# Quantised rows turned by SyncE's DMA transposes, context chunks moved ahead of the evictions, two LoRA tiles ahead of the coefficients

## The chip, the cores and the metric

One NeuronCore of one Trainium2 chip runs the whole kernel. The metric is the device time of one execution in microseconds; three runs of the kernel before give a median of 1277.35 us (1276.79 to 1277.54). The profile below is of one execution, with its own time.

## The reference, cut to what matters

`x` is 2 x 512 rows of 1024, `ctx` is 2 x 1024 rows of 1024. Four steps follow one another; the change lies in the first two.

```python
q1 = fake_quant(layernorm(x), s1, z1)          # (clip(round(x/s + z), 0, 255) - z) * s
q2 = fake_quant(ctx, s2, z2)                   # here ctx stands as a 1024 x 1024 matrix for each batch
x = x + tanh(g_xattn[0]) * (q1 @ q2)
y = layernorm(x)
coeffs = softmax((y.mean(1) @ Wq.T) @ lora_keys.T / sqrt(128))
h = einsum('bsi,eir->bser', y, lora_down)
x = x + tanh(g_ffn[0]) * (y @ W_org.T + einsum('be,bser,ero->bso', coeffs, h, lora_up))
x = x + tanh(g_xattn[1]) * cross_attention(layernorm(x), ctx)   # 32 query heads, 8 key/value heads
x = x + tanh(g_ffn[1]) * two_of_three_experts(layernorm(x))
```

## The kernel before

Each engine has an instruction list written out by hand, and semaphores tie the lists together. An engine takes its list strictly in order, so an instruction that waits holds up all that stand behind it. There are TT = 8 token tiles of 128 rows, TB = 4 for each of the B = 2 batches, and KT = 8 slices of the contraction.

**Front, first part (0 to about 97 us).** TensorE computes the attention's keys and values of both batches from the transposed context (`keys_values`, 16 passes, each raises `kv_step`), in all eight PSUM banks. The context arrives in 32 chunks (`CHUNKS`): T chunks are the transposed context for the keys, split into a bf16 high part (ScalarE, line 1078) and low part (VectorE, L1353); N chunks are the natural context, scaled by ScalarE (L1080), clipped and rounded by VectorE into `Q2` (L1398 and L1400). A ring of six buffers holds them, two in `stage_c` and four in the space of `XTh`; SyncE loads a chunk once the one six places before it is done (`c_done`, L364). Between the chunks VectorE normalises and quantises the eight x tiles (`x_step`, `quantise_x`) into `XQ`, which is the space of `XTl`; ScalarE takes roots (L1086), scales (L1090) and sums each row of `XQ` (`row_sum`, L1097). After batch 0 and batch 1 both engines evict the banks (`kv_out`: ScalarE L1103 and L1106, VectorE L1412 and L1417). In ScalarE's list chunks 26 and later, and in VectorE's list chunks 28 to 31, stand about or behind `kv_out(1)`, and ScalarE's `add_rows` (L1110, adds the row term to x) stand between chunks.

**Front, second part (to about 218 us).** TensorE turns every quantised tile with eight 128x128 transposes into bank 6 or 7 (`turn_quantised`, L694, `xq_turned`); ScalarE copies it to `XTh` (`quantised_out`, L1115, `xq_t`). `column_sums` (L686) multiplies `Q2` by ones in banks 4 and 5; VectorE's `column_terms` (L1496) scales this into `CB`, and GpSimd's `add_columns` (L539) adds it to x (`x_pre`). `quantised_tile(t)` (L718, 16 matmuls) computes q1 q2 for one token tile in banks 0, 1 or 2, 3 (`nat_mm`). VectorE's `quantised_update(t)` adds it to x (L1513, `x_up`), takes the statistics of the new row (L1366, L1371) and the inverse root (L1379 to L1385) and leaves `ln_bias`; ScalarE's `scale_rows(t)` writes the normalised rows (L1196); TensorE's `turn_behind(t)` transposes them into banks 4 and 5 (L706); ScalarE's `turned_out(t)` (L1202) and VectorE's `lo_parts(t)` (L1503) split them into `XTh` and `XTl`. `lo_parts(t-2)` stands inside `quantised_update(t)`, and `turn_behind(t)` waits for `lo_parts(t-1)`, since both use banks 4 and 5.

The adapters follow: `lora_query` (24 matmuls), `lora_scores`, VectorE's `lora_shares` with one Exp on ScalarE, `lora_spread` (L739) and the copy into `cvec` give the coefficients; `lora_hidden(u)` (24 matmuls) gives the eight hidden tiles, which ScalarE and VectorE scale with them (L1214, L1552). Before the change only `lora_hidden(0)` stands ahead of `lora_spread(0)`.

GpSimd splits weights into high and low parts (L507 and L509, one pair for each 128x1024 slice, `wt_done`), in the order of `WT_LAYOUT`: four slices of down, eight of org, four of up, then q and o. SyncE feeds it through two staging buffers (L354). The token tiles of the second step (`token_tile`) start when the up and org slices are split.

Of the kernel before, what the change touches and what calls it, by code (L numbers as in the profile page):

```python
# [42 lines left out]
WT_LAYOUT = [("kv", 4), ("down", 4), ("org", 8), ("up", 4), ("q", 8), ("o", 8)]  # L43
# [15 lines left out]
H_BANK = (7, 6, 7, 6, 1, 6, 7, 2)  # L59
# [57 lines left out]
def build(nc, x, ctx_nat, ctx_t, wts, lora_q, lora_keys, scalars, gate_w, w1, b1, w2, b2, out):  # L117
    with ExitStack() as ctx:
# [65 lines left out]
        XQ = XTl  # L184
        ring = [st[:, :] for st in stage_c] + [XTh[:, :].bitcast(F32)[:, i * D:(i + 1) * D] for i in range(RING - 2)]
# [60 lines left out]
        xq_turned = sem("xq_turned")  # L246
        xq_t = sem("xq_t")
# [100 lines left out]
        def _(sp):  # L348
# [147 lines left out]
        def _(pool):  # L496
# [127 lines left out]
        def _(pe):  # L624
# [58 lines left out]
            def column_sums(b):  # L683
                for h in range(2):
                    for k in range(KT):
                        mm = pe.matmul(bank[4 + h][:, :], onesb[:, :],  # L686
                                       Q2[b][:, k * D + h * HALF:k * D + (h + 1) * HALF], start=k == 0, stop=k == KT - 1)
                mm.then_inc(cs_mm, 1)

            def turn_quantised(t):  # L690
                if t >= 2:
                    pe.wait_ge(xq_t, t - 1)
                for k in range(KT):
                    mm = pe.transpose(bank_b[6 + t % 2][:, k * P:(k + 1) * P], XQ[:, t * D + k * P:t * D + (k + 1) * P],  # L694
                                      identb[:, :])
                mm.then_inc(xq_turned, 1)
# [14 lines left out]
            def quantised_tile(t):  # L711

                pe.wait_ge(xq_t, t + 1)
                if t >= 2:
                    pe.wait_ge(x_up, 2 * (t - 1))
                for h in range(2):
                    for k in range(KT):
                        mm = pe.matmul(pair(t)[h][:, :], XTh[:, k * D + t * P:k * D + (t + 1) * P],  # L718
                                       Q2[t // TB][:, k * D + h * HALF:k * D + (h + 1) * HALF],
                                       start=k == 0, stop=k == KT - 1)  # L720
# [55 lines left out]
            pe.wait_ge(xq_t, TT)  # L776
            lora_query(0)
            quantised_tile(TT - 1)
            turn_behind(TT - 3, 1)
            lora_scores(0)  # L780
            pe.wait_ge(wt_done, WT_AT["org"])
# [7 lines left out]
            lora_hidden(2)  # L789
            pe.wait_ge(h_lo, 2)  # L790
            lora_hidden(3)
            pe.wait_ge(x_up, 2 * TT)
            lora_query(1)
            lora_hidden(4)
            lora_scores(1)
            pe.wait_ge(h_lo, 4)
            lora_hidden(5)
            lora_spread(1)
            lora_hidden(6)
# [265 lines left out]
        def _(act):  # L1065
# [47 lines left out]
            def quantised_out(t):  # L1113
                act.wait_ge(xq_turned, t + 1)
                act.activation(per_tile(XTh)[:, :, t * P:(t + 1) * P],  # L1115
                               bank_b[6 + t % 2].rearrange("p (k n) -> p k n", k=KT), ACT.Copy).then_inc(xq_t, 1)


# [25 lines left out]
            scale_x(4)  # L1144
            kv_out(0)
            chunks(9, 10)
            row_sum(3)
            root(5, 1)
            chunks(10, 12)
            scaled(5)  # L1150
            chunks(12, 15)
            root(6, 0)
            chunks(15, 17)
            scaled(6)
            chunks(17, 19)
            root(7, 1)
            chunks(19, 20)
            scaled(7)
            chunks(20, 22)
# [9 lines left out]
            act.wait_ge(c_done, len(CHUNKS))  # L1169
# [53 lines left out]
            scale_rows(1)  # L1223
            for t in range(2, TT):
                turned_out(t - 2)
                scale_rows(t)
            lora_exp(0)
# [115 lines left out]
        def _(dve):  # L1343
# [131 lines left out]
            chunks(8, 9)  # L1475
            kv_out(0)
            chunks(9, 10)
            x_step(5)
            chunks(10, 15)
            x_step(6)  # L1480
            chunks(15, 19)
            x_step(7)
            chunks(19, 22)
# [400 lines left out]
```

## Time and profile before

| | us |
|---|---|
| median of the runs shown | 1277.35 |
| the profiled execution's own time | 1272.04 |
| its span, first to last instruction | 1270.2 |
| TensorE busy in the span | 1224.8 |

The profiled execution is 5.3 us shorter than the median, and 1.8 us of its time lie outside its span. TensorE is busy for 96% of the span. In the slices of 20 us it is busy 19.9 us in nearly every one from 180 us on; the slices with less lie in the front. An idle time in the timeline is printed behind the instruction that ended it, with what released it. Durations of one form are nearly constant, so a difference of two start times is the safest measure of a step.

### The profile page before, as it was taken

To read this page: it belongs to the slowest core of one execution; us is meant where nothing else is said; L and a number is where in the kernel's file an instruction comes from. 1 tells how busy PE (TensorE), PEld (TensorE's weight loads), DVE (VectorE), ACT (ScalarE), POOL (GpSimd) and SP (SyncE) were. 2 spreads that over 40 slices of the span, in tenths; PEclk is the share of its full clock that TensorE was granted. 3 is DMA by queue.
4 is the path that set the end of the run, shared out by engine and by line. 5 is a ranking of instruction groups with operands and counts; after the bars stand their busy time and mean duration, and the time that the engine had idled before them with its cause. 6 is when DMAs were issued, how large, how long until landed. Compare 5 with 4: busy or idle time off the path is not lost.

```text
span 1270.2 us, 16963 instructions
## 1 busy us (share of the span) xinstructions
PE 1224.8 (96%) x6485; PEld 518.0 (41%) x6568; DVE 821.0 (65%) x1417; ACT 483.9 (38%) x834; POOL 682.2 (54%) x300
## 2 busy tenths in 40 slices
PE   8997889999999999999999999999999999999998
PEld 6564444444444322222222222234444444444444
DVE  7877941333355678999899998516547855737622
ACT  4569321000011266777677767752253010010000
POOL 6004994900023387988889889980074553534510
PEclk9998989999999999999999999999999999999999
DMA  9464232411252334545454545343484342533301
GB/s 354 145 198 149 77 123 67 117 34 34 52 153 75 92 86 86 119 105 118 87 115 108 111 94 107 79 88 60 107 205 123 117 149 91 176 98 100 116 11 55
DMA packets 78317, 139.11 MB, mean 110 GB/s; under 512 B 40608, under 2 KB 50848, under 8 KB 74144
## 3 DMA queue, kind: packets, MB, share of 16 engines
q1 hardware_dynamic: 37392, 91.93, 22.7%
q0 software_dynamic: 4608, 33.56, 13.1%
q10 hardware_dynamic: 36240, 12.60, 5.0%
q8 instruction: 49, 0.80, 0.3%
q14 instruction: 28, 0.23, 0.1%
HBM read 85.49 MB, written 10.49 MB: 76 GB/s over the span
## 4 chain that ended last, share of the span: by engine, by line
PE 70%; DVE 12%; issue 2%; ACT 2%; DMA 2%; POOL 2%; ACTq 0%; SPq 0%; POOLq 0%; DVEq 0%
PE bank L631 45%; PE bank L881 9%; DVE mxp L1624 7%; PE bank L868 6%; PE bank L950 5%; PE bank L913 4%; DVE xn L1614 2%; POOL R L597 1%; PE bank L718 1%; DMA XTh<-xn 1%; DMA stage_pair<-R 1%; DVE XTl L1503 1%; DVE X L1513 0%; POOL stage_pair L597 0%; ACT R L1303 0%
## 5 line engine op out<-in xcount | busy, mean ns | idle before, releaser
L1624 DVE TENSOR_REDUCE mxp<-bank 128x1 f32<-128x512 f32 x512 | 320.5, 679 | 60.3 <-PE bank L868 60.0
L1269 ACT ACTIVATE R<-bank 128x512 f32<-128x512 f32 x512 | 273.9, 602 | 116.5 <-PE bank L950 113.2
L631 PE MATMUL bank<-XTh,R 128*128 128x512 bf16 x875 | 273.8, 382 | 1.9 <-DVE X L1672 1.1
L597 POOL TENSOR_TENSOR R<-R 128x2048 f32<-128x2048 f32 x48 | 218.6, 4555 | 36.5 <-ACT R L1269 34.8
L631 PE MATMUL bank<-R 128*128 128x512 bf16 x941 | 208.2, 379 | 1.0
L631 PE MATMUL bank<-XTl,R 128*128 128x512 bf16 x440 | 167.9, 382 | 2.1 <-ACT R L1327 1.4
L619 POOL TENSOR_TENSOR R<-stage_pair,R 128x1024 bf16<-128x1024 f32 x32 | 75.7, 2380 | 141.7 <-DVE R L1778 84.8
L631 PEld LDWEIGHTS bank<-R 128*128 128x128 bf16 x960 | 93.9, 98 | 113.3
L868 PE MATMUL bank<-R 96*128 96x512 bf16 x352 | 134.6, 382 | 4.7 <-DVE mxp L1624 3.0
L881 PE MATMUL bank<-R,stage_c 128*32 128x512 f32 x1024 | 137.1, 607 | 0.7 <-ACT R L1269 0.7
L950 PE MATMUL bank<-R 98*128 98x512 bf16 x352 | 134.4, 382 | 2.5 <-ACT R L1269 2.2
L631 PEld LDWEIGHTS bank<-XTh,R 128*128 128x128 bf16 x896 | 88.1, 98 | 109.7 <-issue 3.0
L507 POOL TENSOR_TENSOR R<-stage_pair,zero 128x1024 f32 (+1 forms) x35 | 67.2, 1920 | 91.1 <-DMA stage_pair<-wts_in 75.0
L619 POOL TENSOR_TENSOR R<-stage_c,R 128x1024 bf16<-128x1024 f32 x32 | 74.1, 2326 | 54.7 <-DVE R L1778 50.2
L1327 ACT ACTIVATE R<-bank,b1t 128x512 f32<-128x512 f32 x32 | 21.6, 686 | 198.3 <-PE bank L631 198.3
L868 PEld LDWEIGHTS bank<-R 96*128 96x128 bf16 x352 | 34.2, 97 | 112.2 <-DVE mxp L1624 85.5
L509 POOL TENSOR_TENSOR R<-stage_pair,R 128x1024 f32 (+1 forms) x35 | 75.9, 2168 | 5.3 <-POOL R L507 4.7
L1614 DVE RECIPROCAL xn<-p_total 128x128 f32<-128x128 f32 x64 | 59.2, 936 | 29.1 <-POOL xn L579 29.1
L597 POOL TENSOR_TENSOR stage_pair<-R 128x2048 f32<-128x2048 f32 x16 | 73.6, 4601 | 4.3 <-ACT R L1269 3.2
L913 PE MATMUL bank<-R,XTh 128*128 128x512 bf16 x250 | 69.5, 384 | 1.0 <-issue 0.8
L1823 DVE SCALAR_TENSOR_TENSOR X<-xn,TV,X 128x512 f32<-128x512 f32 x32 | 67.4, 2146 | 0.1
L1804 DVE CAST R<-R 128x512 bf16<-128x512 f32 x32 | 17.5, 547 | 74.9 <-ACT R L1327 74.9
(197 smaller groups left out, 1504.3 us busy)
## 6 DMA issues: line engine op xcount, KB each, us to landing
stage_pair<-wts_in SPq DMA_DIRECT2D x35, 512.0 KB, 3.6
R<-R POOLq DMA_DIRECT2D x16, 1024.0 KB, 7.0
stage_pair<-R POOLq DMA_DIRECT2D x16, 1024.0 KB, 7.0
stage_pair<-w_in SPq DMA_DIRECT2D x32, 512.0 KB, 3.6
stage_c<-w_in SPq DMA_DIRECT2D x32, 512.0 KB, 3.6
R<-q_scr SPq DMA_DIRECT2D x48, 128.0 KB, 2.4
XTh<-ctx_t_in SPq DMA_DIRECT2D x11, 512.0 KB, 7.6
XTh<-ctx_nat_in SPq DMA_DIRECT2D x9, 512.0 KB, 4.5
```

What stands on the lines that cost most here:

```text
L509: pool.tensor_tensor(lo, stage_w[stage][:, :], hi, ALU.subtract).then_inc(wt_done, 1)
L597: pool.tensor_tensor(PS[(0, 1, 2, 1)[j]], PB[2 * j % 4], PB[2 * j % 4 + 1], ALU.add).then_inc(p_add, 1)
L619: pool.tensor_tensor(lo[:, cols], stage_e[(n - N_WT) % RING_E][:, :], hi[:, cols], ALU.subtract).then_inc(wt_done, 1)
L631: mm = pe.matmul(o, a, m, start=first and a is ah and bs is bh, stop=last and a is al)
L868: pe.matmul(bank[s_bank(u)][:, :], QS[g % 3][0:96, h * S + qt * P:h * S + (qt + 1) * P], KS[g % 3][0:96, kh * HALF:(kh + 1) * HALF], start ...
L881: mm = pe.matmul(out_bank[h * HD:(h + 1) * HD, :], weights, probs[:, h * S:(h + 1) * S], start=first, stop=last)
L913: mm = pe.matmul(outs[h], a[i][:, cols], b[i][:, k * D + h * HALF:k * D + (h + 1) * HALF], start=k == 0 and i == 0, stop=k == KT - 1 and i ...
L950: pe.matmul(bank[t_bank(g, t)][:, :], KS[g % 3][0:98, kt * P:(kt + 1) * P], QS[g % 3][0:98, h * S:(h + 1) * S], start=True, stop=True).the ...
L1269: act.activation(PB[kt % 4][:, h * S:(h + 1) * S], bank[t_bank(g, t)][:, :], ACT.Exp, scale=float(HD) ** -0.5).then_inc(exp_done, 1)
L1614: dve.reciprocal(rec[:, cols], p_sum[:, cols]).then_inc(rec_done, 1)
L1624: dve.tensor_reduce(mxp[head // REP % 2][:, m, n // 2, n % 2:n % 2 + 1], bank[s_bank(u)][:, :], AX.X, ALU.max).then_inc(s_max, 1)
L1823: dve.scalar_tensor_tensor(out=xh, in0=b2b[:, hc], scalar=TV[:, j * TT + t:j * TT + t + 1], in1=xh, op0=ALU.mult, op1=ALU.add).then_inc(eo ...
```

## The change

* `turn_quantised` and `quantised_out` are gone. SyncE issues eight DMA transposes of `XQ` into `XQT`, the space of `R[2]` (before: the high part of the transposed context, later the high part of org), once `kv_step` has reached 16. They stand ahead of `keys_out(1)` and of the loads of the down weights. Each has a semaphore of its own, on which TensorE's `quantised_tile(t)` waits; VectorE waits for all eight ahead of `quantised_update(2)`.
* ScalarE and VectorE take chunks earlier: two before `kv_out(0)`, up to chunk 29 (ScalarE) and 28 (VectorE) before `kv_out(1)`. `add_rows(0)` to `(3)` stand behind the last chunk, `(4)` and `(5)` behind `scale_rows(2)`, `(6)` and `(7)` behind `scale_rows(3)`.
* `column_sums(1)` uses banks 6 and 7 and moves ahead of `quantised_tile(2)`; `column_sums(0)` still uses 4 and 5.
* `lora_hidden(1)`, in bank 0, stands ahead of `lora_spread(0)`.
* The up weights come ahead of the org weights in the layout, in SyncE's loads and in GpSimd's splits; the org splits wait for all eight quantised tiles. `gate_parts` moves behind `lora_shares(1)`.

```diff
-WT_LAYOUT = [("kv", 4), ("down", 4), ("org", 8), ("up", 4), ("q", 8), ("o", 8)]
+WT_LAYOUT = [("kv", 4), ("down", 4), ("up", 4), ("org", 8), ("q", 8), ("o", 8)]
-H_BANK = (7, 6, 7, 6, 1, 6, 7, 2)
+H_BANK = (7, 0, 6, 7, 1, 6, 7, 2)
+        XQT = R[2]
...
-            load_weights(WT_AT["down"], 2)
+            def turn_x(t):
+                sp.wait_ge(xq_done, t + 1)
+                sp.dma_start_transpose(out=per_tile(XQT)[:, :, t * P:(t + 1) * P],
+                                       in_=XQ[:, t * D:(t + 1) * D]).then_inc(xq_t[t], 16)
+            sp.wait_ge(kv_step, KT * B)
+            for t in range(TT):
+                turn_x(t)
+            keys_out(1)
+            load_weights(WT_AT["down"], 4)
             sp.wait_ge(c_done, len(CHUNKS))
             sp.dma_start(LQW[:, :], lora_q).then_inc(lqw_in, 16)
-            keys_out(1)
-            load_weights(WT_AT["down"] + 2, 2)
+            load_weights(WT_AT["up"], 4)
             load_weights(WT_AT["org"], 8)
-            load_weights(WT_AT["up"], 4)
```

In GpSimd's list:

```diff
-            split_group("org", org_h, org_l)
             pool.wait_ge(k_out, 64)
             pool.wait_ge(x_pre, TT)
             split_group("up", up_h, up_l)
+            pool.wait_ge(nat_mm, TT)
+            split_group("org", org_h, org_l)
```

In TensorE's list, after `keys_values(1)`:

```diff
-            turn_quantised(0)
-            turn_quantised(1)
             pe.wait_ge(v_act, 4)
             column_sums(0)
-            turn_quantised(2)
             pe.wait_ge(k_lo, 8)
-            quantised_tile(0)
-            turn_quantised(3)
-            turn_quantised(4)
-            quantised_tile(1)
-            turn_quantised(5)
-            turn_quantised(6)
+            for t in range(2):
+                quantised_tile(t)
             pe.wait_ge(c_done, len(CHUNKS))
+            column_sums(1)
+            quantised_tile(2)
             pe.wait_ge(cb_done, 2)
-            column_sums(1)
-            turn_quantised(7)
-            quantised_tile(2)
-            pe.wait_ge(cb_done, 4)
             turn_behind(0, 0)
-            for t in range(3, TT - 1):
+            quantised_tile(3)
+            turn_behind(1, 1)
+            for t in range(4, TT - 1):
                 quantised_tile(t)
                 turn_behind(t - 2, t % 2)
+            pe.wait_ge(cb_done, 4)
             pe.wait_ge(lqw_done, 1)
             lora_query(0)
             quantised_tile(TT - 1)
             turn_behind(TT - 3, 1)
             lora_scores(0)
             lora_hidden(0)
+            pe.wait_ge(x_up, 2 * (TT - 1))
+            lora_hidden(1)
             lora_spread(0)
             turn_behind(TT - 2, 0)
             pe.wait_ge(cv_done, 2)
-            lora_hidden(1)
+            lora_hidden(2)
             turn_behind(TT - 1, 1)
```

In ScalarE's list, about `kv_out(1)` and behind it:

```diff
-            chunks(22, 24)
-            for i in range(TB):
-                chunks(24 + 2 * i, 26 + 2 * i)
-                if i == 1:
-                    kv_out(1)
-                add_rows(i)
+            chunks(26, 30)
+            kv_out(1)
+            chunks(30, 32)
+            for t in range(TB):
+                add_rows(t)
...
-            for t in range(TT - 1):
-                quantised_out(t)
-                if t < TB:
-                    add_rows(TB + t)
             scale_rows(0)
-            quantised_out(TT - 1)
             scale_rows(1)
             for t in range(2, TT):
                 turned_out(t - 2)
                 scale_rows(t)
+                if t < 4:
+                    add_rows(2 * t)
+                    add_rows(2 * t + 1)
```

In VectorE's list, the same places:

```diff
-            chunks(22, 24)
+            chunks(23, 29)
+            kv_out(1)
             dve.wait_ge(rowq_done, TT)
             dve.tensor_scalar(rterm[:, :], rowq[:, :], qc[:, 5:6], qc[:, 4:5], ALU.add, ALU.mult).then_inc(rterm_done, 1)
-            chunks(24, 28)
-            kv_out(1)
-            chunks(28, 32)
-            gate_parts()
+            chunks(29, 32)
...
             column_terms(1)
-            dve.wait_ge(xq_turned, TT)
-            for t in range(2, TT - 1):
+            for t in range(TT):
+                dve.wait_ge(xq_t[t], 16)
+            quantised_update(2)
+            for t in range(3, TT - 1):
                 quantised_update(t)
```

## Rows read from the trace of the kernel before

**Rows 1.** The page's first line.
```profile
span 1270.2 us, 16963 instructions
```

**Rows 2.** Stretches: length, busy (instructions) of each engine, PEclk, DMA share, GB/s.
```profile
51.00:97.00 46.00, 43.37 (x287) 28.55 (x289) 37.42 (x72) 30.61 (x39) 0.00 (x0) 0.96 0.57 175
97.00:109.00 12.00, 5.36 (x27) 3.19 (x29) 11.31 (x19) 12.00 (x16) 0.00 (x0) 0.72 0.72 253
109.00:130.70 21.70, 17.77 (x116) 9.22 (x116) 13.47 (x37) 16.38 (x18) 17.23 (x8) 1.00 0.29 98
...
152.00:180.00 28.00, 23.89 (x109) 12.17 (x110) 15.89 (x47) 9.54 (x15) 26.64 (x15) 0.88 0.42 130
```

**Rows 3.** Timeline of PE: start us, us, instruction, idle time before it and releaser.
```profile
53.70 4.14 PE L656 MATMUL bank<-R 128*128 128x512 bf16 x11 [2.40 <-DVE R L1417]
...
103.41 1.87 PE L694 MATMUL bank<-identb,XTl 128*128 128x128 bf16 x16 [6.49 <-DVE V L1412]
...
112.71 0.62 PE L694 MATMUL bank<-identb,XTl 128*128 128x128 bf16 x8 [2.50 <-ACT XTh L1115]
...
170.96 0.59 PE L739 MATMUL bank<-coef,onesf 1*128 1x8 f32 x2 [3.84 <-DVE coef L1541]
```

**Rows 4.** Timeline of DVE.
```profile
51.33 0.69 DVE L1412 COPY V<-bank 128x512 f32<-128x512 f32 x1 [3.29 <-PE bank L662]
...
101.98 1.28 DVE L1412 COPY V<-bank 128x512 f32<-128x512 f32 x2
...
105.58 0.68 DVE L1398 TENSOR_SCALAR XTh<-XTh 128x1024 f32<-128x1024 f32 x1
...
111.77 1.40 DVE L1496 TENSOR_SCALAR R<-bank,qc 128x512 f32<-128x512 f32 x2
116.90 1.41 DVE L1513 SCALAR_TENSOR_TENSOR X<-bank,qc,X 128x512 f32<-128x512 f32 x2 [3.73 <-PE bank L718]
...
123.67 0.16 DVE L1379 RECIPROCAL lnv<-lnv 128x1 f32<-128x1 f32 x1 [3.60 <-ACT lnv L1086]
...
130.57 1.40 DVE L1513 SCALAR_TENSOR_TENSOR X<-bank,qc,X 128x512 f32<-128x512 f32 x2
...
147.67 1.40 DVE L1513 SCALAR_TENSOR_TENSOR X<-bank,qc,X 128x512 f32<-128x512 f32 x2
...
153.36 1.40 DVE L1513 SCALAR_TENSOR_TENSOR X<-bank,qc,X 128x512 f32<-128x512 f32 x2
```

**Rows 5.** The chain that ended last: start us, us, what.
```profile
109.90 1.04 ACT X L1110
...
113.33 3.45 PE bank L718 x16
```

**Rows 6.** Timeline of POOL.
```profile
113.31 9.31 POOL L539 TENSOR_TENSOR X<-X,R 128x1024 f32<-128x1024 f32 x4 [84.81 <-DVE R L1496]
...
130.73 9.30 POOL L539 TENSOR_TENSOR X<-X,R 128x1024 f32<-128x1024 f32 x4
...
218.29 1.89 POOL L507 TENSOR_TENSOR R<-stage_pair,zero 128x1024 f32 x1 [16.06 <-PE bank L631]
```

**Rows 7.** Timeline of ACT.
```profile
136.39 1.25 ACT L1196 ACTIVATE xn<-X,lnv 128x1024 f32<-128x1024 f32 x1 [1.23 <-DVE lnv L1521]
137.53 1.06 ACT L1202 ACTIVATE XTh<-bank 128x512 bf16<-128x512 f32 x2
```

**Rows 8.** Line 1182, DMA transposes of one tile from ACT's queue, later in the kernel.
```profile
L1182 ACTq DMA_TRANSPOSE XTh<-xn x16: 1247/1248/1332, 240.7 to 941.9; - x16
...
DMA to landing us min/median/max: 3.0/3.2/10.1
```

**Rows 9.** DMA queues in 240.7 to 246, two such transposes: packets, MB, share.
```profile
q10 hardware_dynamic: 2112, 0.52, 53.7%
```

**Rows 10.** Part 6 of the page, DMA issues: size, us to landing.
```profile
stage_pair<-wts_in SPq DMA_DIRECT2D x35, 512.0 KB, 3.6
```

**Rows 11.** A stretch of 1 us, columns as in rows 2.
```profile
53.00:54.00 1.00, 0.30 (x1) 0.28 (x3) 1.00 (x3) 1.00 (x3) 0.00 (x0) 0.76 0.00 0
```

More of the change, by code:

```diff
@@ L245, in build @@
         xq_done = sem("xq_done")
-        xq_turned = sem("xq_turned")
-        xq_t = sem("xq_t")
+        xq_t = [sem(f"xq_t{t}") for t in range(TT)]
         kv_step = sem("kv_step")
@@ L685, in column_sums @@
                     for k in range(KT):
-                        mm = pe.matmul(bank[4 + h][:, :], onesb[:, :],
+                        mm = pe.matmul(bank[4 + 2 * b + h][:, :], onesb[:, :],
                                        Q2[b][:, k * D + h * HALF:k * D + (h + 1) * HALF], start=k == 0, stop=k == KT - 1)
                 mm.then_inc(cs_mm, 1)
[L690 to L696, printed above, removed]
             def pair(m):
@@ L711, in quantised_tile @@
             def quantised_tile(t):
-                pe.wait_ge(xq_t, t + 1)
+                pe.wait_ge(xq_t[t], 16)
                 if t >= 2:
@@ L717, in quantised_tile @@
                     for k in range(KT):
-                        mm = pe.matmul(pair(t)[h][:, :], XTh[:, k * D + t * P:k * D + (t + 1) * P],
+                        mm = pe.matmul(pair(t)[h][:, :], XQT[:, k * D + t * P:k * D + (t + 1) * P],
                                        Q2[t // TB][:, k * D + h * HALF:k * D + (h + 1) * HALF],
@@ L779, in _ @@
             turn_behind(TT - 3, 1)
+            pe.wait_ge(const_in, 48)
             lora_scores(0)
-            pe.wait_ge(wt_done, WT_AT["org"])
+            pe.wait_ge(wt_done, WT_AT["up"])
             lora_hidden(0)
+            pe.wait_ge(x_up, 2 * (TT - 1))
+            lora_hidden(1)
             lora_spread(0)
@@ L785, in _ @@
             pe.wait_ge(cv_done, 2)
-            lora_hidden(1)
+            lora_hidden(2)
             turn_behind(TT - 1, 1)
             pe.wait_ge(h_lo, 1)
-            lora_hidden(2)
-            pe.wait_ge(h_lo, 2)
             lora_hidden(3)
             pe.wait_ge(x_up, 2 * TT)
+            pe.wait_ge(h_lo, 2)
             lora_query(1)
@@ L795, in _ @@
             lora_scores(1)
-            pe.wait_ge(h_lo, 4)
+            pe.wait_ge(h_lo, 3)
             lora_hidden(5)
             lora_spread(1)
+            pe.wait_ge(h_lo, 4)
             lora_hidden(6)
@@ L1144, in _ @@
             scale_x(4)
+            chunks(9, 11)
             kv_out(0)
-            chunks(9, 10)
+            chunks(11, 12)
             row_sum(3)
             root(5, 1)
-            chunks(10, 12)
+            chunks(12, 15)
             scaled(5)
-            chunks(12, 15)
+            chunks(15, 17)
             root(6, 0)
-            chunks(15, 17)
-            scaled(6)
             chunks(17, 19)
+            row_sum(5)
+            scale_x(6)
+            chunks(19, 22)
             root(7, 1)
-            chunks(19, 20)
-            scaled(7)
-            chunks(20, 22)
+            chunks(22, 23)
+            row_sum(6)
+            scale_x(7)
+            chunks(23, 26)
             row_sum(7)
             act.wait_ge(rowq_done, TT)
-            chunks(22, 24)
-            for i in range(TB):
-                chunks(24 + 2 * i, 26 + 2 * i)
-                if i == 1:
-                    kv_out(1)
-                add_rows(i)
+            chunks(26, 30)
[3 more added lines that the diff above has]
+                add_rows(t)
             act.wait_ge(const_in, 48)
-            act.wait_ge(c_done, len(CHUNKS))
             def rows_turned(m, t, rooted=False, before_lower=lambda: None):
@@ L1215, in hidden_out @@
                                scale=cvec[:, u:u + 1]).then_inc(h_hi, 1)
-            for t in range(TT - 1):
-                quantised_out(t)
-                if t < TB:
-                    add_rows(TB + t)
             scale_rows(0)
-            quantised_out(TT - 1)
             scale_rows(1)
+            act.wait_ge(c_done, len(CHUNKS))
             for t in range(2, TT):
@@ L1474, in _ @@
             x_step(4)
-            chunks(8, 9)
+            chunks(8, 11)
             kv_out(0)
-            chunks(9, 10)
             x_step(5)
-            chunks(10, 15)
+            chunks(11, 16)
             x_step(6)
-            chunks(15, 19)
+            chunks(16, 20)
             x_step(7)
-            chunks(19, 22)
+            chunks(20, 23)
             quantise_x(7)
-            chunks(22, 24)
+            chunks(23, 29)
+            kv_out(1)
             dve.wait_ge(rowq_done, TT)
             dve.tensor_scalar(rterm[:, :], rowq[:, :], qc[:, 5:6], qc[:, 4:5], ALU.add, ALU.mult).then_inc(rterm_done, 1)
-            chunks(24, 28)
-            kv_out(1)
-            chunks(28, 32)
-            gate_parts()
+            chunks(29, 32)
             def column_terms(b):
@@ L1495, in column_terms @@
                 for h in range(2):
-                    dve.tensor_scalar(CB[:, b, h * HALF:(h + 1) * HALF], bank[4 + h][:, :], qc[:, 3:4], None,
+                    dve.tensor_scalar(CB[:, b, h * HALF:(h + 1) * HALF], bank[4 + 2 * b + h][:, :], qc[:, 3:4], None,
                                       ALU.mult).then_inc(cb_done, 1)
@@ L1573, in _ @@
             lora_shares(1)
+            gate_parts()
             for u in range(JT, B * JT):
@@ L1861 @@
             chunks(a["L0_ffn_lora_down"].transpose(1, 0, 2).reshape(D, ER)),
+            chunks(a["L0_ffn_lora_up"].reshape(ER, D)),
             chunks(a["L0_ffn_W_org"].T),
-            chunks(a["L0_ffn_lora_up"].reshape(ER, D)),
             chunks(a["L1_xattn_Wq"]),
```

5 lines of the change are left out of this document (removed).

## The prediction

> **What bounds the kernel now.** I read the busy times by stage first, then TensorE's timeline for its idle times, the chain of waits to see which engine stands behind each, and the timelines of the other engines to work out what moves. TensorE is busy nearly throughout, so only its idle and low-clock time in the front can be won. Three places matter. (1) After the keys and values of batch 1 TensorE waits 6.49 us for VectorE, which comes to the evictions only at 101.98 because it is still at chunks [rows 3, 4]; the clock then falls (mean 0.72 over 12 us, [rows 2]). (2) From the first `quantised_update` on the chain lies on VectorE: it starts at 116.90, once TensorE has the first tile, loses 3.60 us to a root that stands behind transposed copies in ScalarE's list, and reaches `quantised_update(2)` at 130.57; from there one tile takes 5.69 us (147.67 to 153.36) [rows 4]. (3) At 170.96 TensorE has waited 3.84 us for the coefficients, and goes on at a low clock: 0.88 over 28 us [rows 2, 3]. Behind the front GpSimd is no bound: its last split of org and up ends at 218.29 - 16.06 = 202.23, while TensorE frees it at 218.29 [rows 6].
>
> **The change step by step.** Times are on the trace's axis.
>
> *Chunks before the evictions.* Ahead of `kv_out(0)` VectorE now has two more chunks. It used to wait 3.29 us there for TensorE [rows 4]; chunks 9 and 10 take about 1.15 us each and need ScalarE's half first, so it is 0.4 us late at 51.33 and so are TensorE's evicted banks (97.0 becomes 97.4). Between 51 and 97 VectorE is busy 37.42 of 46 us and ScalarE 30.61 [rows 2]. An N chunk costs VectorE 1.33 us (two instructions as at 105.58, [rows 4]). Before, chunks to 23 were done at 97; the change adds 24 to 28, 5 x 1.33 = 6.7 us, into 8.6 us of idle time. ScalarE adds 26 to 29, some 4.6 us, into 15.4 us. Laid out in order with the loads (issued six chunks earlier, about 4 us to land) VectorE is through at about 94. Both then start the evictions at 97.4 instead of 101.98. Covered by idle time, so nothing is paid; without that cover each chunk costs 1.33 us.
>
> *TensorE restarts.* The two V copies take 1.28 us [rows 4], so `column_sums(0)` runs 98.8 to 102.3: a group of 16 matmuls takes 3.45 us [rows 5]. The gap shrinks from 6.49 to 1.5 us. Tile 0 needs the last low key part, 97.4 + (105.58 - 101.98) + 0.1 = 101.1, and its DMA transpose.
>
> *The DMA transposes.* ScalarE's queue shows the same shape of transfer: 1.25 us to issue, 3.2 us to land in the median [rows 8]. Two of them took 53.7% of the 16 engines for 5.3 us, so 1.4 us each [rows 9]. Tile t therefore lands at 97.4 + 3.3 + 1.4 t: tile 0 at 100.7, tile 7 at 110.5. TensorE takes one per 3.45 us from 102.3, VectorE wants all at 119.65: hidden, with 1.6 us to spare at tile 0 and 9 at VectorE's wait. The bounds are 3.0 and 10.1 us to land; I take 3.3, the median being 3.2. What is queued behind on SyncE are the key stores and the down weights. These are issued about 108.5 and land at 112 to 113 (3.6 us, [rows 10]); GpSimd wants them at 116.3. The 64 TensorE transposes and eight copies fall away, but they mostly lay in waits, so I count nothing for them beyond these start times.
>
> The Trainium skill (VectorE: DVE Perf Modes, The three transpose paths) gives a DMA transpose of one 128x128 block 1309 ns against 390 ns on TensorE, and thus speaks against this edit. By it the 64 blocks would take an estimated 84 us, the last would land at 181, and the sum would come out near 1326 us. The trace does not agree: eight such blocks land in 3.2 us.
>
> *First update.* VectorE: row term 0.2, chunks 29 to 31, 4.0 us, to 105.3; column terms and the release of GpSimd take 113.31 - 111.77 = 1.54 [rows 4, 6], so 106.85. ScalarE has chunks 30, 31 and four `add_rows` of 1.04 us [rows 5] done at 107, the first at 103.7. GpSimd's first sum takes 9.31 / 4 = 2.33 us [rows 6]: `quantised_update(0)` starts at 109.3, not 116.90, a gain of 7.6. The root now stands behind nothing, so 3.60 becomes the 0.27 of an unhindered one: 3.3 more. `quantised_update(2)` starts at 109.3 + (130.57 - 116.90 - 3.3) = 119.65, 10.9 us earlier. TensorE is ahead: tile 1 at 109.2, `column_sums(1)` at 112.7, tile 2 at 116.1.
>
> *A wait that is added.* `add_rows(4)` and `(5)` now stand between `scale_rows(2)` and `turned_out(1)`. Before, the copy followed at once (136.39, 137.53, [rows 7]) and reached VectorE with about 0.1 us to spare. Two times 1.04 us make `lo_parts(1)` 2.0 us late, inside `quantised_update(3)`; `add_rows(6)` and `(7)` do so to the next. Tiles 3 and 4 take 7.7 us each, and 4.0 us of the gain are given back: updates start at 125.35, 133.05, 140.75, and (6) at 146.5 instead of 153.36, 6.9 us earlier.
>
> *Coefficients.* Up to `lora_hidden(0)` all keeps its distance (tile 7, update 7, 6.9 us earlier), so this ends at 160.1. `lora_hidden(1)`, 24 matmuls of 3.45/16 us, makes 5.2 us; the coefficients, which came 3.84 us late, are then there. The 3.84 us go, and so does the low clock behind it: 12% of 28 us is 6.7 us at the lower of the two levels (1.2 against 2.4 GHz), of which about 5.2 were work that would have taken 2.6. Gain 6.4.
>
> *GpSimd.* `add_columns(1)` waits for x row 7, ready at 136.4 (133.05, plus one scaling of 1.14 and two of 1.04), and ends at 140.0, as it did before (130.73 + 9.30 = 140.03, [rows 6]). All splits behind it remain, 62.2 us, so the last ends at 202.3 as before. The down weights, LQW (144.2, wanted at 145.3) and the wait for eight quantised tiles (154, reached at 169) are in time. TensorE wants the last split at 217.8 - 13.3 = 204.5: spare 2.2 us, before 15.6.
>
> *The clock.* In the slower chain TensorE waits 2.7, 3.1 and 3.1 us for `lo_parts` ahead of `turn_behind(1)` to `(3)`; before, 1.2. After 2.40 us of idle time the clock had fallen (0.76 in the next microsecond), after 2.50 us ahead of 112.71 it had not (1.00 over 109 to 130.7) [rows 2, 3, 11]. I take it to fall. The first two tiles have 3 us of cover; the last, tile 6, runs to 145.1 where `lo_parts(3)` is there at 144.2. Price 0.9; bounds 0 and 3.4 (a whole tile at half clock).
>
> **Sum.** 7.6 + 3.3 - 4.0 + 6.4 - 0.9 = 12.4 us. Against the profiled execution, 1272.04 (span 1270.2, [rows 1]): 1259.6. Its time is 5.3 us below the median; the difference is taken over to the median: 1277.35 - 12.4 = 1265.0 us. Nothing behind the front is touched, so what it gains shifts to the end; `gate_parts` (0.3 us) goes where VectorE waits.
>
> **Rivals.**
> 1. *The chunks don't get ahead.* The ring holds six, and each engine waits for the other's half; VectorE's 6.7 us go into 8.6 us of idle time that is cut into many waits. For it: the small surplus. Against: the waits before came from the order itself. If the evictions stay at 101.98, 4.6 us are lost: 1269.6. Chance 0.14.
> 2. *GpSimd becomes the bound.* The org splits now stand last, with 2.2 us to spare. If LQW or down comes late, or `add_rows(7)` does, each microsecond beyond that is paid. With 4 us late: 1266.8. Chance 0.10.
> 3. *Slower: the queue of transposes.* In place of TensorE's turning stands VectorE's wait for all eight ahead of `quantised_update(2)`, with the key stores and down weights behind them. It decides from (119.65 + 12.4 - 97.4) / 8 = 4.3 us for each; below (119.65 - 97.4) / 8 = 2.8 us VectorE doesn't wait at all. For it: one transpose did take 10.1 us to land, and eight in a row from this queue are not in the trace. Against: two in flight took 1.4 us each. At 10.1 us each the last lands at 178.2, 58.6 us late: 1277.35 - 12.4 + 58.6 = 1323.6. Chance 0.07, of which 0.02 near break-even.
> 4. *The change doesn't do what it says.* TensorE's two big waits are only replaced, by the longer waits for `lo_parts` and by GpSimd, whose end stays at 202.3: 1277.3. Against: GpSimd was 15.6 us ahead. Chance 0.03.
>
> **How the numbers follow.** The forecast has 0.66. A measurement can tell about 0.2%, 2.6 us, from no change. Faster: forecast and rivals 1 and 2, 0.90. Within 0.2%: 0.04. Slower: 0.06. Low end: no clock loss gives 1264.1, and if the `add_rows` delays cost less, GpSimd's 2.2 us of spare is the limit: 1261.9, so 1261.5. High end: rival 1 and the other clock bound, 1270. Left out are rivals 3 and 4, one in ten, and a little on either side for errors in the laid-out order.
>
> **What the profile would show.** Right: VectorE's evictions at about 97.4, `quantised_update(0)` at 109.3 and (2) at 119.7; tiles 3 and 4 at 7.7 us and the others at 5.7; eight transposes on SyncE's queue from 97.4, landed by 111; no idle time ahead of `lora_spread(0)`; GpSimd's last org split at about 202 and the token tiles at 205. Wrong: VectorE waiting for a transpose, chunks after 97.4 on VectorE before the evictions, TensorE waiting for GpSimd's last split, or idle time reappearing behind the front.

## The result and the profile after

| | before | after |
|---|---|---|
| median of the runs at the time, us | 1277.07 (4 runs) | 1256.93 (4 runs, 1254.47 to 1259.31) |
| profiled execution, us | 1272.04 | 1259.31 |
| its span, us | 1270.2 | 1257.5 |

The ratio is 0.9866 (95% interval 0.9843 to 0.9890), so the change gains 20.1 us between these medians and 14 to 20 us by the interval. The forecast was a gain of 12.4 us and 1265.0 us, range 1261.5 to 1270: the direction was right, and the time lies 4.6 us below the range. The two profiled executions differ by 12.7 us, which is nearly the forecast; the other 7.4 us are that the profiled execution before lies 5.0 us below its median (1277.07 - 1272.04) and the one after 2.4 us above its own (1259.31 - 1256.93). So the question is not what the change does in one trace, but why the medians lie further apart than the two traces.

The timeline of VectorE in the changed kernel (start us, us, instruction, idle time before it and what ended it), the lines that answer to rows 4:

```profile
51.47 0.69 DVE L1404 COPY V<-bank 128x512 f32<-128x512 f32 x1
...
97.10 1.29 DVE L1404 COPY V<-bank 128x512 f32<-128x512 f32 x2 [3.70 <-PE bank L672]
...
105.29 1.40 DVE L1485 TENSOR_SCALAR R<-bank,qc 128x512 f32<-128x512 f32 x2
109.20 1.41 DVE L1502 SCALAR_TENSOR_TENSOR X<-bank,qc,X 128x512 f32<-128x512 f32 x2 [2.51 <-POOL X L548]
...
119.61 1.40 DVE L1502 SCALAR_TENSOR_TENSOR X<-bank,qc,X 128x512 f32<-128x512 f32 x2
...
125.30 1.40 DVE L1502 SCALAR_TENSOR_TENSOR X<-bank,qc,X 128x512 f32<-128x512 f32 x2
...
129.25 1.29 DVE L1492 TENSOR_TENSOR XTl<-bank,XTh 128x512 bf16<-128x512 f32 x2 [1.82 <-ACT XTh L1195]
...
132.92 1.40 DVE L1502 SCALAR_TENSOR_TENSOR X<-bank,qc,X 128x512 f32<-128x512 f32 x2
...
146.24 1.40 DVE L1502 SCALAR_TENSOR_TENSOR X<-bank,qc,X 128x512 f32<-128x512 f32 x2
```

VectorE is now ready 3.70 us before TensorE ends the keys and values; the evictions start at 97.10 (forecast 97.4), update 0 at 109.20 (109.3), update 2 at 119.61 (119.65), update 6 at 146.24 (146.5). The pair of row additions costs 1.82 us at tile 3 (2.0). The rows of TensorE and GpSimd, beside rows 3 and 6:

```profile
98.49 3.61 PE L696 MATMUL bank<-R,onesb 128*128 128x512 bf16 x16 [1.43 <-DVE V L1404]
...
123.07 1.06 PE L708 MATMUL bank<-identf,xn 128*128 128x128 f32 x8 [2.83 <-DVE XTl L1492]
...
130.69 1.06 PE L708 MATMUL bank<-identf,xn 128*128 128x128 f32 x8 [3.10 <-DVE XTl L1492]
...
138.31 1.23 PE L708 MATMUL bank<-identf,xn 128*128 128x128 f32 x8 [3.10 <-DVE XTl L1492]
139.32 5.18 PE L720 MATMUL bank<-R 128*128 128x512 bf16 x16
144.34 1.04 PE L708 MATMUL bank<-identf,xn 128*128 128x128 f32 x8
...
165.41 0.38 PE L741 MATMUL bank<-coef,onesf 1*128 1x8 f32 x2
```

```profile
106.83 9.28 POOL L548 TENSOR_TENSOR X<-X,R 128x1024 f32<-128x1024 f32 x4 [78.45 <-DVE R L1485]
...
204.96 1.89 POOL L516 TENSOR_TENSOR R<-stage_pair,zero 128x1024 f32 x1 [2.79 <-PE bank L641]
```

The three waits for `lo_parts` are there (2.83, 3.10, 3.10), the clock falls at the last one (tile 6 takes 5.18 us instead of 3.6), and no wait stands ahead of the coefficients' matmuls at 165.41. GpSimd is freed at 204.96 instead of 218.29 [rows 6]: 13.33 us. The forecast had 13.3 less 0.9 for tile 6. Of that 0.9 the trace shows 0.3. VectorE had its low part for the next transposes ready at 143.9 and TensorE began them at 144.34, only 0.5 us later; the update of tile 7, which waits for TensorE, then comes 6.8 us earlier than before, where the update of tile 6 came 7.1 us earlier. VectorE in the changed kernel:

```profile
142.59 1.27 DVE L1492 TENSOR_TENSOR XTl<-bank,XTh 128x512 bf16<-128x512 f32 x2
...
154.12 1.41 DVE L1502 SCALAR_TENSOR_TENSOR X<-bank,qc,X 128x512 f32<-128x512 f32 x2 [1.50 <-PE bank L720]
```

and the same update in the kernel before:

```profile
160.94 1.41 DVE L1513 SCALAR_TENSOR_TENSOR X<-bank,qc,X 128x512 f32<-128x512 f32 x2 [1.19 <-PE bank L718]
```

The DMA transposes:

```profile
L405 SPq DMA_TRANSPOSE R<-XTl x8: 1316/1336/1372, 97.1 to 106.8; - x8
...
DMA to landing us min/median/max: 3.3/3.4/4.4
```

Eight from SyncE's queue land in 3.4 us each, one every 1.4 us. Nobody waits for them. Busy time and clock by stage, columns as in rows 2:

```profile
51.00:97.00 46.00, 43.90 (x292) 28.64 (x290) 41.07 (x79) 33.37 (x41) 0.00 (x0) 0.96 0.63 218
97.00:109.00 12.00, 10.57 (x50) 4.81 (x50) 9.17 (x15) 9.43 (x12) 2.17 (x1) 1.00 0.94 160
152.00:180.00 28.00, 28.00 (x144) 14.07 (x143) 13.70 (x32) 9.84 (x15) 26.63 (x15) 1.00 0.42 130
```

Of the low clock of rows 2, that behind 97 and that behind 170 are gone. The one behind 51 us is not (0.96).

Behind the front one of the prediction's signs of being wrong is there. TensorE's longest wait between 205 us and the end is one for GpSimd at the experts' weights, which the trace of before does not have (first line: changed kernel, second: the line with before's longest single wait behind its front; us in total, number of waits, longest):

```profile
PE bank L641 <- POOL R L629: 4.5, 1, 4.5
```

```profile
PE bank L950 <- ACT R L1269: 2.8, 3, 2.2
```

Other waits are shorter in exchange: from GpSimd's release to the end it is 1052.5 us (1257.5 - 204.96) against 1051.9 (1270.2 - 218.29), so 0.6 us of the 13.33 are lost again.

### The profile page after: what moved, and what is told of

Its sections match the earlier page's. It is cut to its first block, busy times and chain, and to the rows that moved or that the text cites. A ratio compares the mean times of both kernels' runs of the same rounds, so it can differ in the third digit from the quotient of the medians.

```text
span 1257.5 us, 16924 instructions
## 1 busy us (share of the span) xinstructions
PE 1222.9 (97%) x6504; PEld 512.1 (41%) x6504; DVE 821.9 (65%) x1417; ACT 476.4 (38%) x826; POOL 681.7 (54%) x300
## 4 chain that ended last, share of the span: by engine, by line
PE 79%; DVE 12%; DMA 2%; POOL 2%; ACT 2%; issue 1%; ACTq 0%; SPq 0%; POOLq 0%; DVEq 0%
PE bank L641 46%; PE bank L879 9%; DVE mxp L1616 8%; PE bank L866 6%; PE bank L948 5%; PE bank L911 5%; PE bank L666 3%; PE bank L672 3%; DVE xn L1606 2%; DMA stage_c<-w_in 1%; DMA R<-R 1%; POOL R L607 1%; POOL R L629 1%; PE bank L720 1%; POOL X L548 1%
## 5 line engine op out<-in xcount | busy, mean ns | idle before, releaser
L641 PE MATMUL bank<-XTh,R 128*128 128x512 bf16 x896 | 279.3, 381 | 4.7 <-POOL R L629 4.5
L641 PE MATMUL bank<-XTl,R 128*128 128x512 bf16 x448 | 170.7, 381 | 0.0
L1084 ACT ACTIVATE lnv<-lnv 128x1 f32<-128x1 f32 x32 | 6.5, 202 | 158.7 <-DVE lnv L1365 138.3
```

What stands on the lines that cost most here:

```text
L641: mm = pe.matmul(o, a, m, start=first and a is ah and bs is bh, stop=last and a is al)
```

## The experiments

All times are medians of whole executions unless a profile is named. The runs were taken in several sets, on different chips, each with executions of the kernel before beside it: 65 of these, the first four included, lie between 1268.7 and 1279.0 us, median 1273.3. A comparison with the kernel before uses its own set; one with the changed kernel uses its 1256.0 from the first set below, so it carries the difference between sets as well.

**Both kernels again.** No edit.

> The kernel before, unchanged. Theory A (the front gives 13.3 us in every execution; the rest of the 20 us between the medians is a stall that some executions have and others not, in the stage of the expert weights): single executions spread over 1272 to 1278, and an execution near 1277 shows, against the profiled one of 1272, some 5 us more TensorE waiting behind 900 us and none in the front. Theory B (the front itself varies): the extra waiting or low clock lies ahead of 220 us.

> The changed kernel, unchanged. Its front is expected to end at 204.5 to 205 us again (GpSimd freed at 204.96 in the first profile) in either theory. Theory A: without the 10.35 us load ahead of 925 us and the 4.5 us that TensorE then waits for GpSimd, the span is near 1253; the median of its runs stays 1255 to 1258 and the difference to the kernel before 17 to 21. Theory B: the front's end moves by microseconds between executions.

Measured: 1273.54 (12 runs, 1268.86 to 1274.04) and 1256.0 (6 runs, 1252.51 to 1259.36); the other 21 executions of before in this set have 1273.85. The changed kernel's ratio is 0.9853 (0.9825 to 0.9881). So 1277 was the upper part of a spread that the kernel before has, and the gain is near 17 to 18 us: ten executions of the changed kernel have a median of 1256.6. Both profiled executions of the changed kernel (1259.31, 1259.01) are at the top of its spread. Their front ends agree to 0.1 us, and r1's front ends 0.85 us earlier than that of the first profile, though its execution is 1.9 us longer: the 2.75 us lie behind the front, as theory A has it for the kernel before. TensorE's wait for line 1672 is longer there, 1.1 us in the first line (before), 3.1 in the second (r1_before_again):

```profile
PE bank L631 <- DVE X L1672: 1.1, 1, 1.1
```

```profile
PE bank L631 <- DVE X L1672: 3.1, 1, 3.1
```

Over all whole-kernel profiles the part behind GpSimd's release takes 1048.7 us (r11) to 1054.7 us (r1), so both theories keep something. The new wait of 4.5 us for GpSimd is 3.6 us in r2 and 0.2 us in r11, the profile with the shortest part behind the front. The cut kernels below say where the difference of the medians arises, and this says that single executions also vary behind the front. Its share in the difference of the medians was not measured by itself.

**The fronts alone.** The edit puts a return into each engine's list ahead of the token tiles, and SyncE writes x out. SyncE's part:

```diff
+            sp.wait_ge(wt_done, WT_AT["q"])
+            sp.wait_ge(h_lo, B * JT)
+            sp.wait_ge(x_up, 2 * TT)
+            sp.wait_ge(k_out, 64)
+            for t in range(TT):
+                sp.dma_start(out[t], X[:, t * D:(t + 1) * D]).then_inc(x_out, 16)
+            sp.wait_ge(x_out, 16 * TT)
+            return
```

> The kernel before cut off behind the front: everything from the token tiles of the second step on is left out, and SyncE writes x out once the hidden tiles and the up and org splits are done. Theory A (the front gives 13.3 us in every execution, the rest of the difference between the medians arises where the experts' weights come in): the executions agree within 1 us, the front ends at 217.4 to 218.3 in the profile. Theory B (executions differ in the front, where the TensorE clock falls in one of several gaps): they spread over 3 us or more.

> The changed kernel cut off at the same place. Theory A: 13.3 us below r5_front_before, with a spread under 1 us. Theory B: up to 18 us below in the median, since the changed front has cover for a fallen clock and the front before has none.

> r6_front_after once more, for another profiled execution beside the timed ones. Theory: if its profile shows no fall at 51 us, its evictions of batch 1 come 43.95 us after those of batch 0 instead of 45.6 and it takes 217.5 as the median; with the fall 219.3 to 219.5. Rival: without the fall it is still 2 us above the median, then the profiling costs that.

Measured: 235.07 (233.73 to 235.63) for the old front. The new one gave 217.51 in the first set, five executions between 217.41 and 217.85 and the profiled one at 219.47. In the second it was the other way round: 219.38, five executions between 219.12 and 219.80 and the profiled one at 217.84. So the new front has two times, 217.5 and 219.4, and it lies 15.7 to 17.6 us below the old one. The gain of the medians, 17 to 18 us, thus arises in the front for the most part, as theory B has it. The spread does not: the old front spans 1.9 us, less than the 3 us that theory B called for, and the new one 2.4 us, while the whole kernels span 10.4 us (65 executions) and 6.9 us (ten). Two profiles say what the two times are. The clock from 50 to 60 us, in the profiled execution of r6_front_after (219.47), with the fall:

```profile
50.00:60.00 10.00, 7.76 (x45) 4.55 (x43) 9.75 (x22) 8.54 (x14) 0.00 (x0) 0.83 0.68 228
```

and in that of r18_front_after_again (217.84), without it, followed by lines of its VectorE timeline:

```profile
50.00:60.00 10.00, 7.74 (x52) 4.85 (x51) 9.74 (x22) 8.57 (x14) 0.00 (x0) 1.00 0.66 225
```

```profile
51.10 0.69 DVE L1414 COPY V<-bank 128x512 f32<-128x512 f32 x1
...
95.00 1.29 DVE L1414 COPY V<-bank 128x512 f32<-128x512 f32 x2 [2.01 <-PE bank L680]
```

Without the fall behind the gap at 51 us the evictions of batch 1 start 43.9 us after those of batch 0, with it 45.6 (97.10 - 51.47; 45.6 in every profile of the new order that has the fall). In the old order it is 50.65 us with the fall (101.98 - 51.33, [rows 4]) and without it (the profile of r1_before_again):

```profile
51.63 0.69 DVE L1412 COPY V<-bank 128x512 f32<-128x512 f32 x1 [3.31 <-PE bank L662]
...
102.28 1.28 DVE L1412 COPY V<-bank 128x512 f32<-128x512 f32 x2
```

There VectorE was late anyway and hid the fall; TensorE only waited longer (8.04 instead of 6.49 us). The new front is bound by TensorE at this point, so whether the clock falls makes 1.7 us. In the executions without a profile only the mean clock of the whole front is known. It is 0.953 to 0.962 in the five at 219.1 to 219.8, and 0.966 or 0.967 in three of the five at 217.4 to 217.9, but 0.959 and 0.960 in the other two: that each execution's time follows from this one fall is likely and not shown.

**Moving the gap at 51 us.** In the first pass of batch 1 TensorE does the value part first, and both engines evict the value banks first (the lines on TensorE and ScalarE; VectorE's are like the latter).

```diff
+                if again:
+                    values_part()
+                    return keys_part()
...
-                for i in (0, 1, 2, 3, 4, 5) if b == 0 else (4, 5, 0, 1, 2, 3):
+                for i in (4, 5, 0, 1, 2, 3):
```

> The changed kernel cut off behind the front (as r6_front_after), and in the first pass of batch 1 TensorE does the value part ahead of the key part, with ScalarE and VectorE evicting the value banks first after batch 0. Theory: the clock fell at the gap of 2.1 to 2.4 us at 51 us in the profiles of all kernels with the new chunk order, costing them 1.7 us, and VectorE has no time left there to cover it, as it had before; with a gap of 1.2 us the clock stays, the evictions of batch 1 start 2.5 us earlier than in r6_front_after's profile (94.2 instead of 96.7), and the profiled execution is 2.5 us shorter, the others about 1 us (217.5 becomes 216.5). Rival: the fall is not tied to that gap, and it comes elsewhere: 0 to 1 us.

> r5_front_before with the value part first, as in r9_front_values. Theory: in the old order VectorE reaches the evictions of batch 1 50.65 us after those of batch 0 whether the clock fell at 51 us or not, so the edit is worth nothing here: 235.1 +- 0.5. Rival: it gives 1 us or more, as in the new order.

Measured: 216.57 us (216.51 to 216.91) in the new front, one time instead of two, with the clock at 1.00 behind the gap, now 1.25 us, and the evictions at 93.49. That is 0.9 below the better and 2.8 below the worse time of r6 and r18: the theory holds. In the old front 233.71 (233.02 to 234.16), 1.4 below r5. The theory had 0.5 at most there, so by the number the rival's "1 us or more" came. Its profile has the evictions 50.65 us behind those of batch 0 again (101.29 - 50.64), so the cover is as the theory has it, and the 1.4 are not gained at this place. r5 ran in another set, on another chip; where the 1.4 come from is open. The 15.7 above compares across the same two sets and is no surer than that; the 17.6 is from one set.

**Where along the front.** The same kind of cut, first ahead of TensorE's work on the quantised tiles, then behind the last normalised row, without adapters.

> The kernel before cut off behind its last chunk (left out: turning, quantised tiles, updates, adapters and all that follows; x is written out as it is). Theory: VectorE's chain sets its end at 111.5, whatever the clock does, so the executions agree within 1 us.

> The changed kernel cut off at the same place, without the DMA transposes. Its end is ScalarE's fourth row addition at 106.5 with a fall at 51 us and 104.9 without. Theory (other executions lack the fall): 6.6 us below r13 in the median. Rival (they have it as the profiled one): 5.0 us.

> The kernel before cut off behind the last normalised row, with the adapters, the up and the org weights left out. By the profiles the update of tile 6 stands at 153.4 in the kernel before and at 146.2 in the changed one. Theory: the difference to r16 is 7.2 us plus the 1.7 us of the fall at 51 us, 8.9, and what is left to 17.6 (8.7) arises at the coefficients. Rival: 11 us or more, then executions of the kernel before lose clock in the gaps at 97 and 110 us beyond the profiled one.

> The changed kernel cut off as r15_rows_before. Theory: 8.9 us below it; rival: 11 us or more.

Measured: 124.67 and 119.95 (4.7 apart: the rival's 5.0); 185.34 and 178.45 (6.9 apart, 2.0 below the theory's 8.9; the rival is out). Here the profile of the new order had the fall at 51 us both times, and both pairs show no more than the profiles do: the extra 1.7 us, which the theory expected of executions without the fall, did not come in either. What is left to the 15.7 to 17.6 of the whole front, 8.8 to 10.7, would arise at the coefficients, where the first two profiles show 6.5 (13.33 less the 6.8 at the update of tile 7). That is 2.3 to 4.2 more. The lower figure is that of the slower time of the new front, the one with the fall, so the fall does not explain these 2.3 us. Part of them may be that the cut kernels lack work that keeps TensorE busy; this was not separated.

**The parts one by one.** First the LoRA tile alone on the kernel before, and undone in the changed one (cut from the edit: the banks and waits of the later hidden tiles):

```diff
             lora_hidden(0)
+            pe.wait_ge(x_up, 2 * (TT - 1))
+            lora_hidden(1)
             lora_spread(0)
```

> The kernel before with lora_hidden(1) in bank 0 ahead of the coefficients and nothing else. Theory: the 3.84 us wait goes and the low clock behind it (2.6 us), so the front ends 6.4 us earlier, at 211.9, and the time is 6.4 us below that of before (ratio 0.995). Rival: the clock falls elsewhere or the coefficients are still late, then 0 to 4 us.

> The changed kernel with lora_hidden(1) put back behind the coefficients. Theory: TensorE waits 3.6 to 3.9 us for them again and goes on at the low clock, so the time is 6.4 us above the changed kernel's (1262.4 against 1256.0), front end at 211. Rival, after r4_lora_alone (3.6 us in the front's end, 6.3 in the medians): the low clock is not paid, 3.8 us.

Measured: 1267.52, 6.3 us below before (ratio 0.9948, 0.9930 to 0.9967), and 1264.28, 8.3 above the changed kernel of another set, where 6.4 was expected. The wait is back there (profile of r11_no_lora_ahead):

```profile
163.24 0.59 PE L741 MATMUL bank<-coef,onesf 1*128 1x8 f32 x2 [4.49 <-DVE coef L1530]
```

The step's 6.4 us fits the first median, and is low for the second. The profiles are less tidy. That of r4_lora_alone also shows a place of low clock in the old front that the profile of before did not have, behind the gap ahead of the third turned tile:

```profile
109.00:116.00 7.00, 3.78 (x19) 1.59 (x18) 4.28 (x8) 6.30 (x8) 2.34 (x2) 0.85 0.44 134
```

```profile
118.93 1.41 DVE L1515 SCALAR_TENSOR_TENSOR X<-bank,qc,X 128x512 f32<-128x512 f32 x2 [5.41 <-PE bank L718]
```

VectorE waits 5.41 us for TensorE's first tile instead of 3.73 [rows 4], with no cover: 1.7 us. And r1 had paid less for the coefficients than the first profile of before, since its clock was less low behind them (before, then r1_before_again):

```profile
165.00:180.00 15.00, 10.94 (x44) 5.82 (x44) 5.10 (x17) 4.59 (x7) 14.34 (x8) 0.77 0.46 136
```

```profile
165.00:180.00 15.00, 11.29 (x53) 5.74 (x52) 5.13 (x19) 5.20 (x8) 14.34 (x8) 0.89 0.44 136
```

So the front of r4 ends only 3.6 us ahead of r1's (213.81 against 217.44 at GpSimd's release), and 2.8 us of the 6.4 between these two executions lie behind the front. That the medians differ by 6.3 us is therefore in part luck.

Then the chunk order, alone on the kernel before and undone in the changed kernel:

```diff
-            chunks(24, 28)
-            kv_out(1)
-            chunks(28, 32)
+            chunks(23, 29)
+            kv_out(1)
...
+            chunks(29, 32)
```

> The kernel before with the new chunk order on ScalarE and VectorE (row additions 0 to 3 behind the last chunk) and TensorE's turning kept. Theory: evictions at 97.1, first copy of a quantised tile at 107.5 instead of 111.6, first update 4.5 us earlier at 112.4, the 3.6 us wait for the root stays; 4.5 us below the kernel before. Rival (the parts need each other: the gap ahead of the turned tiles only moves from ahead of the evictions to behind them): under 2.5 us.

> The changed kernel with the chunk order of before on ScalarE and VectorE. Theory: the evictions start at 102 again, the first update at 115.5 instead of 109.2, all the rest shifts with it, so the time is 6.2 us above the changed kernel's. Rival (GpSimd's chain bounds the front, or the gap brings a low clock on top): less than 4 or more than 7.

Measured: 1268.4, 5.9 below before (4.5 expected, ratio 0.9952, 0.9935 to 0.9969), and 1263.68, 7.7 above the changed kernel (6.2 expected; over 7 was the rival's range, so the number is the rival's). Its six executions lie between 1260.05 and 1267.26. In the profile of r7 the front takes 213.78 - 53.95 = 159.8 us from VectorE's first evictions to GpSimd's release, against 204.96 - 51.47 = 153.5: 6.3. Its first evictions come 2.5 us later than in the changed kernel for another reason, a low clock at the start (0.83 over 10 to 20 us, 1.00 in the changed kernel). The further 1.4 would fit what the theory of the cover adds in executions without a fall at 51 us, but they were not measured apart from this spread.

Then the DMA transposes one by one:

```diff
                 sp.wait_ge(xq_done, t + 1)
+                if t > 0:
+                    sp.wait_ge(xq_t[t - 1], 16)
```

> The changed kernel with each DMA transpose issued only when the one before it has landed. Theory: at 3.4 us each the last lands at 97.1 + 27.2 = 124.3, so quantised_update(2) starts 4.7 us later than at 119.6, the down weights land at about 126 instead of 113, GpSimd catches up at its wait for the rows, and the time is 4.7 us above the changed kernel's, still 8 below that of before. Rival: GpSimd, 10 us late at its first down split, does not catch up and bounds the front: 8 to 10 us above.

Measured: 1262.16, 6.2 above the changed kernel, where 4.7 was expected and the rival had 8 to 10; between the profiled executions it is 2.7 and at GpSimd's release 3.3 (208.29 - 204.96), so 3 us of the 6.2 have no place in the profiles. In its profile VectorE does wait for a transpose, and GpSimd for the down weights behind them, and later VectorE waits once more for GpSimd:

```profile
122.26 1.41 DVE L1504 SCALAR_TENSOR_TENSOR X<-bank,qc,X 128x512 f32<-128x512 f32 x2 [2.73 <-DMA R<-XTl]
...
137.50 1.41 DVE L1504 SCALAR_TENSOR_TENSOR X<-bank,qc,X 128x512 f32<-128x512 f32 x2 [1.83 <-POOL X L550]
```

So the third rival's mechanism exists: at 3.1 us a transpose it costs, above the 2.8 us that it named. In the change they come every 1.4 us, and it never acts.

**Better versions.** All row additions behind the last chunk, where ScalarE was idle, and then the value part first as well:

```diff
-            for t in range(TB):
+            for t in range(TT):
                 add_rows(t)
...
                 scale_rows(t)
-                if t < 4:
-                    add_rows(2 * t)
-                    add_rows(2 * t + 1)
```

> The changed kernel with all eight row additions behind the last chunk. Theory: in the changed kernel the pairs behind scale_rows(2) and (3) delay VectorE by 1.8 to 2 us each. Here both go (4.0 less 0.4), GpSimd ends its splits at about 196, the updates of tiles 3 and 4 take 5.7 us, the front ends at about 201, and the time is 3.6 to 4 us below the changed kernel's. Rival: GpSimd's splits are what the token tiles wait for, then it stays at 202 and at most 2 us come.

> r3_rows_early with the value part first, as in r9_front_values, the whole kernel. Theory: 1 to 2.5 us below r3_rows_early (1252.8), so 1250.3 to 1251.8, the best version so far.

Measured: 1252.84 (ratio to before 0.9826, 0.9799 to 0.9853), 3.2 below the changed kernel, and 1251.86 (0.9824, 0.9805 to 0.9842) in another set, which cannot be told from it (1 to 2.5 us less was expected). The added wait is gone and GpSimd, which ended 2.79 us ahead of TensorE, is now 5.30 ahead (profile of r3_rows_early):

```profile
200.69 1.89 POOL L516 TENSOR_TENSOR R<-stage_pair,zero 128x1024 f32 x1 [5.30 <-PE bank L641]
```

Both are faster than the changed kernel: no more than one of its ten executions (1252.51) lies among theirs, which reach from 1249.96 to 1253.77.

## Why the prediction was wrong

- **Chunks ahead, evictions, first update, root, added wait, coefficients, GpSimd.** Each step came out within 0.5 us in the profile, and 7.6 + 3.3 - 4.0 + 6.4 = 13.3 is the 13.33 that was measured at GpSimd's release in the profiled executions. For the profiled execution the sum gave 1272.04 - 12.4 = 1259.6, and it took 1259.31. The rivals about chunks, GpSimd in the front and the transposes did not happen. Eight transposed blocks land in 3.4 us and follow one another every 1.4 us. The Trainium skill (VectorE: DVE Perf Modes, The three transpose paths) has 1309 ns for one 128x128 block. The trace of after does not agree either.
- **The clock.** The 0.9 us for tile 6 was too much: the clock fell, but TensorE was only 0.5 us behind VectorE, and 0.3 us were paid.
- **Behind the front.** "Nothing behind the front is touched, so what it gains shifts to the end" holds to 0.6 us between the two profiles, by luck in part: a wait of 4.5 us for GpSimd is new and other waits are shorter, and the same stretch differs by up to 6 us between the profiles of all whole kernels.
- **The step that failed** is the last: "Its time is 5.3 us below the median; the difference is taken over to the median". It gives the changed kernel an execution-to-median distance that was measured on the other kernel, with three executions. The runs showed that the profiled execution of the changed kernel is 2.4 us above its median (2.7 over ten executions), and that of the kernel before 1.3 us below the median of 65, not 5.3. So the medians differ by 16.7 us (1273.3 - 1256.6) where the profiled executions differ by 12.7; of the first comparison's 20.1 us the other 3.4 are spread.
- **What makes the 4 us between traces and medians** is shown in part. First, "without that cover each chunk costs 1.33 us" looked at VectorE alone. The row at 53.70 [rows 3] showed a fall of the clock that VectorE's lateness hid; once VectorE is early, TensorE sets the end of the first part, and each execution without that fall gains 1.7 us more. Both profiles of the changed kernel had it, and so had seven of the ten profiles with the new chunk order and the keys first, so how often the other executions lack it is not known. Second, the old front could lose 1.7 us at the gap ahead of 112.71, where the profiled execution had lost nothing; one of six profiles of the old order (r4) did, and the new front has no such gap. With both, 13.3 becomes 15 to 16.7. Third, single executions vary by several us behind the front, which these two terms leave out. The sum of the first two shows that the size fits; the shares stay open.
- **The range.** Its low end, 1261.5, allowed for none of this, since it took 13.3 us as all that "no clock loss" can give, from a starting median of 1277.35.

## What to carry to other kernels

When an edit takes away the slack of one engine, list what that slack was hiding on the others, low clock included, and price the state without it from both sides. A forecast for a median needs the spread of the executions of both kernels: here a difference of two traces was good to half a microsecond in each step and still missed the medians by 4 us. Two us of instructions, put twice between a scaling and the copy that the next engine waits for, cost 3.8 us of delay in VectorE's updates; moved behind the last chunk they cost nothing that the medians show (3.2 us less).

## What the runs showed of the hardware

- Whether the clock falls behind a gap of 2.1 to 2.7 us at the same place of the same kernel differs between executions: in 11 of 17 profiles with the keys first in batch 1 it fell (mean 0.83 over 50 to 60 us), in 6 it did not (1.00), and gaps of 2.10 to 2.32 us are on both sides. In the new order it makes 1.7 us at the evictions. With the values first the gap is 0.9 to 1.25 us, and it did not fall in any of three profiles.
- DMA transposes of 128x1024 bf16 in a row from SyncE's queue take 1.34 us each to issue and 3.3 to 4.4 us to land, with TensorE at full clock beside them (1.00 over 97 to 109 us). Each issued only when the one before has landed, they take 1.23 us and 3.0 to 3.2 us, and one comes every 3.1 us (r8).
